# Layernorm, attention, mixture of experts on one core: tile 1's routing started in the last attention batch

## What is computed

```python
x = x + _layernorm(attention(_layernorm(x)))   # 16 heads of 8, softmax over 256 keys, biases on q, k, v, o
x = x + _layernorm(ffn(_layernorm(x)))

# ffn: 32 experts of 64 in 8 groups of 4, and one shared expert of 256
logits = x @ gate_w.T
scores = sigmoid(logits)
sc = scores + e_bias
group_scores = top_k(sc by group, 2)[0].sum(-1)
group_idx = top_k(group_scores, 4)[1]
topk_idx = top_k(where(group in group_idx, sc, 0.0), 6)[1]
topk_w = scores[topk_idx]; topk_w = topk_w / (topk_w.sum(-1) + 1e-20) * 2.5
h = relu(x @ up_w.T)**2 * combine            # combine: topk_w scattered to 32 experts
out = h @ down_w.T + relu(x @ shared_up_w.T)**2 @ shared_down_w.T
```

## Time and profile before

| what | value |
|---|---|
| time, median of 3 runs | 501.53 us (501.43 to 502.6) |
| time of the profiled execution | 502.27 us |
| its span | 500.4 us |
| PE busy | 460.5 us, 92% of the span |
| DVE, ACT, POOL busy | 78%, 71%, 50% |
| stages | attention to 257 us, tile 0 of the experts from there to 287 us |

### The profile page before, as it was taken

One profiled execution on the slowest core, in us unless ns is written; L12 is line 12 of the kernel. 1 busy time (PEld: TensorE's weight loads), 2 busy tenths in 40 slices (PEclk: granted clock), 3 DMA queues, 4 the chain that ended last, 5 costly groups with the idle time before them and its releaser, 6 DMA issues.

```text
span 500.4 us, 10661 instructions
## 1 busy us (share of the span) xinstructions
PE 460.5 (92%) x3328; PEld 266.2 (53%) x3328; DVE 390.0 (78%) x1000; ACT 354.2 (71%) x707; POOL 248.1 (50%) x583
## 2 busy tenths in 40 slices
PE   2457999999999999999999899999999999999994
PEld 2212444444444454454456566666666666666662
DVE  3688888899999989989648678695977869496453
ACT  2324788888888888888676677768688776866552
POOL 7045323335757835322733617748293764626351
PEclk9999999999999999999899899999999999999998
DMA  7543344444455445430043344455362545546431
GB/s 207 164 144 102 101 132 133 138 137 143 128 148 151 150 124 151 121 101 3 3 175 126 107 151 133 168 182 182 106 213 87 167 155 189 176 114 207 128 104 42
DMA packets 49047, 67.45 MB, mean 135 GB/s; under 512 B 3808, under 2 KB 35808, under 8 KB 48992
## 3 DMA queue, kind: packets, MB, share of 16 engines
q1 hardware_dynamic: 48992, 66.78, 42.4%
HBM read 51.17 MB, written 15.20 MB: 133 GB/s over the span
## 4 chain that ended last, share of the span: by engine, by line
PE 75%; DVE 10%; issue 7%; POOL 4%; ACT 3%; DMA 0%; POOLq 0%; DVEq 0%; ACTq 0%
PE pO L1295 10%; PE pS L1235 9%; PE pY L1376 8%; PE pS L1376 8%; PE pS L1360 6%; PE pS L1362 6%; PE pS L1361 6%; DVE mneg L953 5%; PE pS L1241 3%; PE pX L1220 2%; PE pY L1312 2%; PE pY L1324 2%; PE pX L1223 2%; DVE q_rest L933 1%; PE pX L1215 1%
## 5 line engine op out<-in xcount | busy, mean ns | idle before, releaser
L953 DVE TENSOR_REDUCE mneg<-pS 128x2 f32<-128x512 f32 x256 | 162.2, 685 | 16.5 <-PE pS L1235 16.1
L742 ACT ACTIVATE probs<-pS 128x512 f32<-128x512 f32 x256 | 141.4, 596 | 26.9 <-PE pS L1241 25.4
L1235 PE MATMUL pS<-qk 48*128 48x256 bf16 x512 | 87.6, 289 | 14.9 <-DVE mneg L953 8.4
L827 ACT ACTIVATE h_ring<-r 128x512 f32<-128x512 f32 x104 | 64.5, 625 | 35.7 <-DVE r L1084 27.4
L1360 PE MATMUL pS<-qk,up_hi 128*128 128x512 f32 x144 | 88.7, 616 | 0.0
L1241 PE MATMUL pS<-qk 51*128 51x256 bf16 x512 | 86.6, 280 | 0.5 <-ACT probs L742 0.3
L1295 PE MATMUL pO<-probs,vv 128*32 128x256 f32 x1024 | 72.9, 392 | 0.0
L1235 PEld LDWEIGHTS pS<-qk 48*128 48x128 bf16 x512 | 33.7, 96 | 65.9 <-DVE mneg L953 44.9
L1084 DVE SCALAR_TENSOR_TENSOR r<-pS,probs 128x512 f32<-128x512 f32 x64 | 43.6, 689 | 29.1 <-PE pS L1362 28.1
L1362 PE MATMUL pS<-qk,up_lo 128*128 128x512 f32 x144 | 57.2, 397 | 0.0
L1361 PE MATMUL pS<-qk,up_hi 128*128 128x512 f32 x144 | 57.0, 396 | 0.0
(11 more groups left out here) (191 smaller groups left out, 819.3 us busy)
## 6 DMA issues: line engine op xcount, KB each, us to landing
c_ring<-c_scratch SPq DMA_DIRECT2D x32, 512.0 KB, 4.0
probs<-c_scratch SPq DMA_DIRECT2D x32, 512.0 KB, 3.9
qk<-qk_scratch SPq DMA_DIRECT2D x64, 192.0 KB
qk_scratch<-q_parts SPq DMA_DIRECT2D x16, 192.0 KB, 2.3
qk_scratch<-k_parts SPq DMA_DIRECT2D x16, 192.0 KB, 2.7
qk_scratch<-q_parts SPq DMA_DIRECT2D x16, 128.0 KB, 2.7
qk_scratch<-k_parts SPq DMA_DIRECT2D x16, 128.0 KB, 2.3
out_x<-probs SPq DMA_DIRECT2D x7, 256.0 KB, 4.7
```

Of the source, the lines that this page charges most:

```text
L742: nc.scalar.activation(probs[j][:, hh], s2_bank(n)[:, :, :], ACT.Exp, scale=SCALE).then_inc(exp_done, 1)
L827: nc.scalar.activation(h_ring[:, (n - at) % HRING], r_sb[n % URING][:, :], ACT.Square).then_inc(sq_done, 1)
L953: nc.vector.tensor_reduce(mneg[u % 2][:, :, hh, k], pS1[n % S1_RING][:, :].rearrange("p (a s) -> p a s", a=TH), AX.X, ALU.max, negate=True ...
L1235: return mm(pS1[n % S1_RING][:, T * th:T * (th + 1)], qp[slot][rows, k, P * th:P * (th + 1)], kp[slot][rows, k, :], start=True, stop=True)
```

## The change

The x1 of tile 1 is transposed after step 0 of the last attention batch on PE and copied by ACT after the exponential of s = 2. Its logits stand in step 6, and their exponential after that of s = 14. `route` for tile 1 starts after `rect` 0 of tile 0, and takes k = 0, 1, 2, 3, 4, 6, 7, 9 in place of 3, 4, 5, 6, 7, 8, 9, 11. `root_score` stands after the square of k = 2 and not 5, `transpose_c` and `keep_cT` at k = 11 and not 13. On POOL the third low part of tile 0 now comes after `root_of_sum`. No instruction is added or taken away, and tiles 1 to 7 are as before.

```diff
-ROUTE_AT = ((3, 4, 5, 6, 7, 8, 9, 11),
+ROUTE_AT = ((0, 1, 2, 3, 4, 6, 7, 9),
             (1, 2, 3, 4, 5, 6, 7, 9))
-SPREAD_AT = (13, 11)
+SPREAD_AT = (11, 11)
...
                 if i == 0:
                     low(i, 1)
-                    low(i, 2)
                 if i + 1 < NTILE:
                     root_of_sum(i + 1)
                 if i >= 1:
                     low(i, 1)
+                if i == 0:
+                    low(i, 2)
...
+                    if s == 2 and last:
+                        keep_xT(1)
                     if s == 9 and last:
                         keep_cT(0)
+                    if s == 14 and last:
+                        exp_logits(1)
...
-                    if i == 0 and k == 1:
-                        keep_xT(1)
                     if i + 1 < NTILE:
-                        if k == (2 if i == 0 else 0):
+                        if k == 0 and i >= 1:
                             exp_logits(i + 1)
-                        if k == (5 if i == 0 else 3):
+                        if k == (2 if i == 0 else 3):
                             root_score(i + 1)
...
+                    if j == 0 and last:
+                        pe.wait_ge(mT_kept, NU)
+                        transpose_x1(1)
                     if j == 4 and last:
-                        pe.wait_ge(mT_kept, NU)
+                        pe.wait_ge(xT_kept, 2)
                         transpose_c(0)
...
+                        if last:
+                            logits(1)
...
-                        if i == 0 and k == 1:
-                            pe.wait_ge(cT_kept, 1)
-                            transpose_x1(1)
-                        if k == (2 if i == 0 else 0):
+                        if k == 0 and i >= 1:
                             logits(i + 1)
```

## The result

The changed kernel takes **504.33 us** in the median of 10 runs (501.81 to 505.24), the kernel before 501.87 in the same session (501.43 to 503.97, 10 runs). The ratio is 1.0045, 95% interval 1.0026 to 1.0064: **slower by 0.45%**. The forecast of 500.5 had the wrong sign, and 504.33 lies above its range. The profiled execution took 503.24 us.

A forecast was written before the change was run, and what follows sets the result against it. PE, busy 92% of the span, was taken as the bound. Tile 1 starting 1.85 us earlier, less 0.85 for half a clock fall, gave -1.0 us: 501.53 becomes 500.5, range 498.5 to 503.0.

The forecast's parts named there:

- The attention batch: Last attention batch, 15: the added transpose, logits and copy make the attention products end 1.2 us later, at 258.35.
- Start of tile 0: Up block 3 of tile 0 at 259.05, 0.85 us ahead of before; DVE starts `rect` 2 at 261.5.
- The wait behind the table load: PE waits 1.3 us before `down_block` 3, from 264.1 to 265.4, for ACT's square behind the table load.
- `rect` 6 at 266.8: DVE in tile 0: summing its earlier busy time, less two `rect`, puts the start of `rect` 6 at 266.8.
- The second wait: PE waits for `onT` before the projection of batch 15: 1.5 us taken, with ends of 0.15 and 1.95.
- Both holds of the forecast: DVE held by POOL: `comb` by `residual1`, wait then 1.05 us; possibly `root_c` by `low` of block 5, another 0.9.
- the upper end: The wait before the projection of batch 15 if both `comb` and `root_c` are held: 1.95 us.
- The rest up to tile 1: From the projection of batch 15 to tile 1's first up block: 16.84 us without the 2.10 and 1.72, 13.0.
- The clock: Old fall of 1.72 us after the 2.10 us wait removed; a new one after 1.5 us counted half, 0.85.
- A second one behind step 5: PE's wait for `onT` before the projection of batch 15, due at 271.0: taken at 1.5 us, between 0.15 and 1.95.
- Rival (b): Slower by the clock: tile 0 waits of 1.3 and 1.95 us, a 1.72 us fall behind each, 503.5 us; chance 0.15.

The follow-up runs named there:

- e11_again: The changed kernel itself, run and profiled once more with nothing altered: 505.02 us, a ratio of 1.0058 to the kernel before.
- e3_onT6: The changed kernel with ACT's copy to `onT` of batch 15 behind the square of block 6, not 7: 501.20 us, 0.9982 of before.
- e8: The changed kernel with later routing steps in tile 0, the root behind square 4, POOL's `residual1` behind the power: 499.11 us, 0.9947 of before.

## Why the prediction was wrong

Point by point, predicted and then measured, in the profiled execution of the changed kernel.

- **The attention batch**: +1.2 us forecast. From the projection of batch 13 to the end of the attention products it is 258.22 - 242.53 = 15.69, before 257.14 - 243.11 = 14.03: +1.66. About 0.3 of this is not the change's but the missing fall at 237: in e11_again, which had it as before had, the stretch is 258.84 - 243.48 = 15.36, +1.33. The transpose took 0.59 to the next start (245.15 to 245.74) and not 0.42, and a wait for an exponential came, 0.16 at 248.83. Right.
- **Start of tile 0**: up block 3 at 259.05; it is 259.03. `rect` 2 at 261.5; it is 261.19. Right, but that closely by luck: this execution was 0.58 us ahead of before's at the projection of batch 13. From the end of the attention products the two are 0.81 and 2.97 us away, where 0.70 and 3.15 were forecast.
- **The wait behind the table load**: 1.3 us from 264.1; it is 1.11 from 264.15. Right, and it costs nothing by itself, since the second one is set by DVE and ACT.
- **`rect` 6 at 266.8**: it is 267.71. Here the first step fails. The sum to 269.47 took steps 2 and 3 with the durations that they had before, where `g_best` ran beside nothing (0.18). The change puts it 0.03 us behind POOL's `low` of block 2.
- **The second wait**: 0.15 to 1.95, taken at 1.5. It is **2.89**, from 271.23. Both holds of the forecast came (`comb` ended at 271.05, `root_c` at 272.41), so the chain is the upper end, 1.95, plus the copy's 1.1 us, less the 0.23 by which PE came later than forecast: 2.8 of the 2.89. The forecast had found the instructions that could be held by their two SBUF inputs. A copy has one. None of the 16 copies `g_best` and `e_best` in the trace of before was held, but one row of it gave the sign: `score` (L1018), with one SBUF input, took 0.43 us at 261.48 and ended 0.09 behind POOL's `low` (260.55, 1.27 us long), where it took 0.22 at 236.70.
- **The rest up to tile 1**: 13.0; it is 14.29 from the projection to the first up block of tile 1 at 288.41, which is 12.58 and a fall of 1.71.
- **The clock**: this term failed twice. It took half a fall for the changed kernel, where all three traces have at least a whole one, and of the untraced runs nearly all. And it credited the change with the removal of a whole fall, since the one trace of before had one; three more show that before pays it in about half of its executions. It should have been about +0.85 and was -0.87.

The sum by measured terms: the attention batch +1.66. From the end of the attention products to tile 1's logits it is 31.82 against 31.87, -0.05: the waits of 1.11 and 2.89 eat all that the old 2.10, the 0.48 and the moved transpose and logits gave free. Both numbers hold a whole fall, and before pays only about half of one on average, which is another +0.85. Together +2.46 us, and +2.46 was measured. That they agree to the hundredth is luck: the half rests on four traces (the mean clocks would give 1.0 for it), with e11_again the first two terms are +1.33 and +0.29, and the medians of two sessions differ, 2.46 and 2.84. The step of the prediction that failed is "A second one behind step 5", a wait taken at 1.5 us that is 2.89 since the copy's hold was no term of it, and then the clock, by 1.7. These two are 3.1 of the 3.5 us between the forecast's -1.0 and the +2.46.

Rival (b) had the sign, the place and nearly the time (503.5), and its point of decision was right: the second wait passed the old 2.10 us and the fall came. Its two falls were wrong; the one behind the first wait did not come in any trace. So that it came near in time is partly luck: a fall too many stands in it for the hold and the half fall that it lacks.

The runs show the missed term first: a copy with one SBUF input is held until POOL's instruction ends, 1.27 us in place of 0.17, and half of that if POOL's instruction is halved. The Trainium skill, page "SBUF — State Buffer", section "Who interferes with whom", says it ahead of time: a copy whose operands meet certain conditions can enter a mode that uses both port pairs and then contends with GpSimd, as an instruction with two SBUF inputs does, and whoever issues first has the shared pair for its whole instruction. By that rule the term would have been in the sum. The pair in e3_onT6, where `comb` started first and was free, agrees with its second half. The copies and the multiplies that were held here agree with it; one row below does not. The price is then the rest of the other instruction's time, which the rows of before had.

## What to carry to other kernels

Before moving VectorE's work, lay its new places beside GpSimd's instructions, and count every copy within SBUF, not only instructions with two inputs, as held until the end of an elementwise GpSimd instruction on SBUF that started ahead of it. If the place can't be changed, cut the GpSimd instruction: two halves took 0.14 to 0.19 us more than the whole here, and three such cuts gave back 3.4 us, half of it a clock fall. Better still was another order: putting only ACT's root back gave 3.6 us, and e8's places 5.0. And one trace of the kernel before shows that a clock fall can come, not that it always does; take more than one before crediting a change with its removal.

## What the runs showed of the hardware

- Held DVE instructions, with their own time and the longest: the copy of 128x16 0.17 and 1.28 us, that of 128x24 0.18 and 0.92, the multiplies of two 128x128 0.29 and 1.35 (`comb`) and 0.37 and 1.47 (`root_c`). Each of them ended 0.02 to 0.25 us behind POOL's instruction, whether it had started 0.03 or 0.74 us behind that one's start. `comb` started 0.09 us ahead of POOL once, in e3_onT6, and was not held.
- Not held: `g_score` of the changed kernel, with two SBUF inputs, took 0.19 us at 262.01, inside POOL's power of 128x4 (261.60 to 262.64), which reads SBUF too. By the rule above it should have been held until 262.64; why it was not stays open.
- TensorE's granted clock (2.4 GHz at 1.00, 1.2 at 0.50) behind a wait in tile 0: down after 2.21, 2.89, 2.90 and 2.91 us, after 2.10 to 2.11 in two of four traces, not after 1.60, 1.41, 1.20 or 1.12. Three matmuls of no use in the wait kept it up. In tile 0 a fall lost 1.7 us each time but one, where it lost 3.4. The fall at 237 came in 11 of the 17 traces, of before and of changed kernels alike, with 1.7 us lost but in e3_onT6, 3.4. What sets either stays open.
